# Patch copies of a deformable convolution issued from one queue, ahead of the stores, with the offsets' part of the schedule shifted

## What is computed

```python
# mixing, on g = group_norm(x), per image, p and q over the 1024 pixels
xn = g / max(norm_over_channels(g), 1e-8)
s  = relu(einsum('bcp,bcq->bpq', xn, xn)) ** 2
gx = einsum('oc,bcp->bop', W, g) + b
x1 = x + einsum('bpq,bcq->bcp', s, gx)
# deformable convolution, on h = group_norm(x1); 4 groups, 9 taps
offset = conv3x3(conv3x3(h, w1, b1), w2, b2)      # 4 * 9 * 2 = 72 channels
val    = bilinear samples of h at (pixel + tap + offset), zero outside
out    = x1 + relu(einsum('ogck,bgckhw->bohw', wd, val))
```

## Time and profile before

| what | value |
|---|---|
| median of three runs | 514.45 us |
| the profiled execution, its own time | 515.51 us |
| its span, first to last instruction | 513.8 us |
| TensorE (PE) busy | 428.8 us, 83% |
| VectorE (DVE) busy | 344.2 us, 67% |
| ScalarE (ACT) busy | 224.7 us, 44% |
| GpSimd (POOL) busy | 140.7 us, 27% |
| mean granted TensorE clock | 0.947 of full |

### The profile page before, as it was taken

How to read it: one execution, slowest core, us unless ns; L and a number is a source line. 1 busy time by engine, 2 the same in 40 slices (tenths; PEclk the granted TensorE clock), 3 DMA queues, 4 the chain that set the end, 5 groups by cost and what they waited for, 6 DMA issues and landing times.

```text
span 513.8 us, 9711 instructions
## 1 busy us (share of the span) xinstructions
PE 428.8 (83%) x3881; PEld 304.9 (59%) x3881; DVE 344.2 (67%) x582; ACT 224.7 (44%) x404; POOL 140.7 (27%) x179
## 2 busy tenths in 40 slices
PE   2899799967998988779998987878798976888886
PEld 2666465734665656557665654657565654666665
DVE  4619996499988983954657992745979538199400
ACT  2046133224565453414655453314765333178640
POOL 3266441343872102102763101101210101031100
PEclk9999799997999989989999989879998987999999
DMA  3400000201111113011101112011210121023211
GB/s 122 169 1 1 1 1 1 46 1 21 22 22 22 22 22 65 6 40 31 33 15 27 22 22 56 23 33 41 43 24 20 25 64 33 20 52 64 42 33 33
DMA packets 22187, 17.23 MB, mean 34 GB/s; under 512 B 1981, under 2 KB 20669, under 8 KB 22141
## 3 DMA queue, kind: packets, MB, share of 16 engines
q1 hardware_dynamic: 21884, 16.07, 12.9%
q10 hardware_dynamic: 256, 0.52, 0.7%
HBM read 3.74 MB, written 3.28 MB: 14 GB/s over the span
## 4 chain that ended last, share of the span: by engine, by line
PE 58%; DVE 24%; ACT 7%; issue 5%; DMA 3%; ACTq 2%; SPq 1%; DVEq 0%
PE psB L719 13%; PE psB L506 12%; PE psA L586 8%; DVE wpix L1342 6%; PE psV L695 5%; PE psA L506 5%; PE psT L672 5%; ACT wcell L897 3%; DVE tent L1323 2%; PE psT L662 2%; DMA hwin<-hwin 2%; PE psA L562 2%; DVE tent L1317 2%; DVE combo L1135 2%; ACT val L910 2%
## 5 line engine op out<-in xcount | busy, mean ns | idle before, releaser
L897 ACT ACTIVATE wcell<-psT 128x512 f32<-128x512 f32 (+1 forms) x160 | 83.4, 552 | 82.3 <-PE psT L672 73.6
L1342 DVE TENSOR_TENSOR wpix<-tent 128x512 f32<-128x512 f32 (+1 forms) x160 | 107.1, 720 | 16.0 <-PE psT L672 15.0
L672 PE MATMUL psT<-ident,wpix 128*128 128x128 f32 x576 | 86.5, 283 | 14.5 <-ACT wcell L897 13.5
L672 PEld LDWEIGHTS psT<-ident,wpix 128*128 128x128 f32 x576 | 66.9, 144 | 38.8 <-issue 28.7
L447 POOL COPY strips<-hring 128x256 f32<-128x256 f32 x64 | 43.3, 702 | 155.8 <-PE psT L662 155.8
L424 POOL TENSOR_TENSOR sim<-rel 128x512 f32<-128x512 f32 x48 | 60.3, 1276 | 62.4 <-ACT rel L858 62.4
L719 PE MATMUL psB<-val,wd_sb 128*128 128x256 f32 x288 | 73.5, 412 | 3.6 <-issue 3.6
L719 PEld LDWEIGHTS psB<-val,wd_sb 128*128 128x128 f32 x288 | 57.7, 206 | 15.6 <-issue 7.2
L695 PE MATMUL psV<-wcell,hwin 64*32 64x144 f32 x2048 | 48.5, 300 | 13.3 <-DMA hwin<-hwin 13.3
L910 ACT ACTIVATE val<-psV 128x576 f32<-128x576 f32 x64 | 44.0, 688 | 34.2 <-PE psV L695 22.7
L506 PE MATMUL psB<-g_p 128*128 128x512 f32 x144 | 44.6, 448 | 6.7 <-DVE g_p L1075 6.7
(11 more groups left out here) (166 smaller groups left out, 498.0 us busy)
## 6 DMA issues: line engine op xcount, KB each, us to landing
hwin<-hwin SPq DMA_DIRECT2D x64, 128.0 KB, 2.5
out<-yout SPq DMA_DIRECT2D x16, 128.0 KB, 1.8
x_all<-x SPq DMA_DIRECT2D x1, 1536.0 KB, 8.9
off_scr<-sim SPq DMA_DIRECT2D x4, 288.0 KB
combo<-sim SPq DMA_DIRECT2D x20, 32.0 KB
val<-w SPq DMA_DIRECT2D x1, 576.0 KB
wd_sb<-wd SPq DMA_DIRECT2D x1, 576.0 KB
x_all<-x SPq DMA_DIRECT2D x1, 512.0 KB, 3.5
```

The costliest lines, as they stand in the source:

```text
L672: last = pe.transpose(bank[:, at:at + P], wpix[:, t % 2, k, 2 * h:2 * h + 2, :].rearrange("p g q -> p (g q)"), ident[:, :])
L897: act.activation(wcell[:, t % 2, taps[0]:taps[-1] + 1, :, :].rearrange("q k h p -> q (k h p)"), bank[:, 0:len(taps) * G // 2 * P], ACT.Cop ...
L1342: dve.tensor_tensor(w, ty, tx, ALU.mult).then_inc(s["weights_done"], 1)
```

## The change

It does the following.

- SyncE issues the crossings of tiles 0 to 6 first, then all nine patch copies of the next batch and the save, the crossing of tile 7, and then all four stores. ScalarE issues patch copies only in the prologue.
- In `STEADY` the second convolution's combinations come one slot later, both convolutions' products (`conv`) come one slot later, and so do the output rows and the wrap; the turns of the offsets move from slots 60 and 61 to 64 and 66, and extremes from 66 to 69. The first weights of the next batch go from slot 62 to 66.
- In the prologue the extremes of batch 0 leave the table and are reduced at slot 12 of batch 0. Batch 2's diagonal goes to a buffer of its own (`ends_out`, which holds `orelu` and `yout` later), so it no longer waits for extremes. `high`, `low` and `diagonal` of batch 2 come one slot sooner, and some steps of batch 1's mixing come sooner.
- Batch 1's borrowed tiles are laid out in two halves by how long they are needed; the first evacuation of weights then waits for the mixing products, and only the one of tile 1 for the scaled sums.

```diff
-        LEAD = dict(mean=31, dev=31, var=33, norm=34, combine=(35, 46), high=(35, 46), conv=(40, 51), wrap=57,
-                    shift=57, turn={59: (0, 1), 61: (2, 3)}, extremes=65)
-        STEADY = dict(mean=23, dev=24, var=25, norm=28, combine=(29, 42), high=(30, 43), conv=(35, 48), wrap=54,
-                      shift=56, turn={60: (0, 1), 61: (2, 3)}, extremes=66)
+        LEAD = dict(mean=31, dev=31, var=33, norm=34, combine=(35, 46), high=(35, 46), conv=(40, 51), wrap=57,
+                    shift=57, turn={59: (0, 1), 61: (2, 3)}, extremes=None)
+        STEADY = dict(mean=23, dev=24, var=25, norm=28, combine=(29, 43), high=(30, 44), conv=(36, 49), wrap=55,
+                      shift=None, turn={64: (0, 1), 66: (2, 3)}, extremes=69)
...
-        SECOND = {26: (0,), 32: (3,), 34: (1, 2, 4), 38: (6,), 46: (7,), 49: (9,), 57: (10, 12, 13), 58: (15, 16),
+        SECOND = {26: (0,), 30: (3,), 34: (1, 2, 6), 35: (4,), 38: (7,), 49: (9,), 57: (10, 12, 13), 58: (15, 16),
                   60: (18, 19), 62: (21, 22), 63: (25,), 64: (26,)}
...
-        LEAD_WEIGHTS, FIRST_WEIGHTS = 60, 62
+        LEAD_WEIGHTS, FIRST_WEIGHTS, LEAD_EXTREMES = 60, 66, 12
...
                 sp.wait_ge(s["off_wrapped"], 2 * b + 2)
-                shift_taps(sp, range(BY_SYNC))
+                shift_taps(sp, range(K if b else BY_SYNC))
...
             for b in range(B):
-                for t in range(ROWT - 2):
+                for t in range(ROWT - 1):
                     cross(b, t)
                 if b + 1 < B:
                     shift_offsets(b + 1)
-                cross(b, ROWT - 2)
-                store(b, 0)
                 cross(b, ROWT - 1)
-                for m in range(1, 4):
+                for m in range(4):
                     store(b, m)
...
                 if b == 0 and t == 0 and idx == 0:
+                    act.wait_ge(s["mix_done"], 2 * QT)
+                if b == 0 and t == 1 and idx == 0:
                     act.wait_ge(s["scaled_done"], 4)
...
                 if what == "diagonal":
                     dve.wait_ge(s["inv2_done"], b + 1)
-                    if b >= 2:
+                    if b >= 3:
                         dve.wait_ge(s["extremes_done"], 2 * (b - 1))
```

More of the change, by code:

```diff
@@ L191, in mix_deform_kernel @@
         acc = spare[:, 2 * G * P + C:2 * G * P + C + K * P]
-        orelu = sb("orelu", [P, 2, HALF // 2])
-        yout = sb("yout", [P, 2, HALF // 2])
+        ends_out = sb("ends_out", [P, 2, HALF])
+        orelu, yout = (ends_out[:, i, :].rearrange("p (j n) -> p j n", j=2) for i in range(2))
         psT = pb("psT", [P, 2, BANK])
@@ L251, in mix_deform_kernel @@
                        27: ("diagonal",), 33: ("bias",)}
[L252 to L253 removed]
+        PREP_THIRD = {57: ("normalise", "square"), 58: ("norms", "invert"), 59: ("bias",), 63: ("high",), 64: ("low",),
+                      65: ("diagonal",)}
         PREP = {55: ("normalise", "square"), 57: ("high", "low"), 58: ("norms", "invert"), 59: ("bias",),
[L255 to L256 removed]
+                70: ("diagonal",)}
+        SECOND = {26: (0,), 30: (3,), 34: (1, 2, 6), 35: (4,), 38: (7,), 49: (9,), 57: (10, 12, 13), 58: (15, 16),
                   60: (18, 19), 62: (21, 22), 63: (25,), 64: (26,)}
@@ L1438, in batch_steps @@
                             add_out(b, 0)
+                        if b == 0 and n == LEAD_EXTREMES:
+                            find_extremes(0)
                         if b + 2 < B:
```

26 lines of the change are left out of this document (13 added, 13 removed).

## The result

The changed kernel takes 496.55 us (median of 4 runs, 494.72 to 498.97), the kernel before 514.20 beside it; the ratio is 0.9652 with a 95% interval of 0.9598 to 0.9707. That is 17.7 us less, where the forecast had 21.8 less, and the time lies inside the range. The profiled execution took 497.49 us, its span is 495.8, so against the profiled execution of before (515.51, span 513.8) the span is 18.0 shorter.

The account below looks back on a forecast made before the run. PE's own work, plus its standstills and lower clock, was taken as the bound. Terms 9.2 + 5.2 + 5.9 + 2.8 + 1.2 - 3.8 - 1.0 - 2.1 + 2.4 + 2.0 = 21.8 gave 492.6 us, range 487 to 504.

Parts of the forecast that it names:

- Stores behind the crossings: Last tile of a batch: shorter `hwin` waits gain 9.2 us, and no half clock behind them gains 5.2.
- The copies leave ScalarE: Around `dconv` 0: PE's wait gains 5.9 us, the slow first group 2.8, batch 0's waits 1.2.
- The new wait: PE waits for SyncE's nine patch copies before the offsets' turn: 1.9 us in batches 1 and 2, 3.8 lost.
- The windows' turns: Tiles 6 and 7: PE's wait of 0.40 ahead of the windows' turn goes, 2.4 us gained.
- Convolutions one slot later: Both convolutions: the wait of 0.94 grows to about 3.0, 2.23 becomes about 1.5; lag 0.7 per batch, 2.1 us lost.
- I set them equal: Convolutions: a clock fall behind the 3.0 us wait stands against the one before, so no net clock term.
- Batch 0's square: Batch 0: the square waits for output rows coming one turn and the lag later, 1.0 us lost.
- The end of the prologue: Prologue: extremes' move gains 2.3 us, exchanged mixing steps taken as -0.3; together 2.0 gained.
- the first: Rival: lengthened and shortened convolution waits both cool PE, 5 us more lost, 497.6 us; chance 0.2.
- The second: Rival: PE stays at 1.2 GHz from the new wait to the batch's end, 498 to 500.9 us; chance 0.1.
- The third: Rival: patch copies land 2 to 4 us later, PE waits in three batches, 499 to 505 us; chance 0.1.
- the fourth: Rival: SyncE's nine issues each take ScalarE's slowest 1.45 us, so slower, 518.2 us; chance 0.02.
- The fifth: Rival: tile 7's crossing waits for its windows behind the offsets' turn, 9.2 and 5.2 not gained, 507.0 us; chance 0.03.

Follow-up runs that it names:

- The single edit: Kernel before with only store 0 put behind tile 7's crossing: 501.39 us, ratio 0.9729.
- The list alone: Changed kernel with only the old table of batch 1's mixing steps in the prologue put back: 493.34 us, ratio 0.9552.
- the kernel with the old slots alone: Changed kernel with the convolutions' slots put back (combining 29 and 42, high half 30 and 43, convolution 35 and 48, wrap 54): 493.56 us, ratio 0.9563.
- the last kernel: Changed kernel with the old prologue mixing order and old convolution slots, plus the offsets' turns moved to slots 66 and 67: 490.04 us, ratio 0.9526.

## Why the prediction was right, and where not

Its sign, its bound (PE) and its main terms held; 17.7 us came where 21.8 were forecast. The terms that missed are the prologue's, batch 0's square and the convolutions', and the last two missed in opposite ways. Point by point, all from the profiled execution:

- *Stores behind the crossings*, 9.2 + 5.2: the four waits are 0.94, 0.94, 0.97 and 0.94, so 9.5 gained; sample and convolution behind them are back to 0.72 and 4.15 in three batches, 5.7 gained. The single edit gave 14.2 of the 14.4. Right.
- *The copies leave ScalarE*, 5.9 + 2.8 + 1.2: all three came. `dconv` 0, from its start to the next turn and without the turns among its groups, took 5.40 and 5.29 and now 3.99, so 1.4 and 1.3 gained, as forecast. Right, and shown to need the later turns beside it.
- *The new wait*, 1.9 in each of two batches, none in batch 0: measured 2.25, 1.85 and none. In batch 1 the issues were a little slower (0.73) and the landing a little sooner (1.8). It cost 1.4 us of clock in batch 1 (7.34 us from the turn to the tail's convolution, 322.53 to 329.87) and none in batch 2 (5.92, 410.02 to 415.94).
- *The windows' turns*, 2.4: the waits ahead of them in tiles 6 and 7 are gone. Right. Three of the six stand inside the convolutions' stretches measured here.
- *Convolutions one slot later*, a lag of 0.7 a batch: wrong in sign for two batches. It was 1.4 lost in the first convolution less 0.7 gained in the second. The first half was right: 1.47 and 1.46 lost in batches 0 and 1, and 3.03 in batch 2. The step that failed is the gain of 0.7 in the second, 1.1 with its wait ahead of the windows: it was 2.91, 2.62 and 2.83. Of that 1.5 in each batch is clock. "I set them equal" was said of the falls behind the two waits, but the one behind 2.23, seen before in all three batches (4.37, 4.00 and 4.46 for twelve matmuls that now take 3.4), did not come behind 1.51 in any.
- *Batch 0's square*, -1.0: mis-sized. From the windows' turn to the first part of `dconv` it is 12.13 instead of 8.17, so -4.0: the wait grew from 0.52 to 2.01, and 2.6 more went to the norms at half clock, which the term had left out. It is the price of the later slots.
- *The end of the prologue*, +2.0: this is the step that failed most. "The exchanged mixing steps fill PE's wait of 2.63", from +0.7 to -2.2, "taken -0.3". They did fill that wait (it is 0.97 now), but the mixing that they took away left PE with 0.70 us of work in the four from 78 to 82, a wait of 4.11 and half clock behind it (6.83 for 4.61), and GpSimd's squares came to lie beside VectorE's combinations and doubled them. The list alone gives 3.2 us back. The "2.3 gained" by the extremes was too much as well: they did leave VectorE's chain, but with the old list about 1.1 of it arrived. Batch 0 began 2.9 us later (126.77 for 123.91) instead of 2.0 earlier.

The same sum by stretches, which add up without a gap (us, from PE's start times in the two profiled executions; a loss is negative; the six waits ahead of the windows are split over the third and the sixth row):

| stretch | forecast | measured |
|---|---|---|
| start to the windows' turn in the middle of batch 0 (159.13, 162.70) | 2.0 | -3.6 |
| first convolutions, three batches | -4.2 | -6.0 |
| second convolutions, with the wait ahead of the windows behind them | 3.3 | 8.4 |
| from there to `dconv` 0: batch 0, with the square and norms | -1.0 | -4.0 |
| the same in batches 1 and 2 (the copies leave ScalarE) | 5.9 | 6.0 |
| `dconv` 0 to the tail's `dconv`: `hwin` waits, slow groups, new wait | 12.1 | 13.2 |
| the tail's `dconv` and the sample behind it | 3.7 | 4.3 |
| everything else | 0 | -0.3 |
| sum | 21.8 | 18.0 |

So it is partly luck that the total missed by only 3.8: 5.6 too much in the first row and 4.8 in the second and fourth stand against 5.1 too little in the third.

Of the rivals, the first (the convolutions lose 5 us more by the clock) came with 1.1 us in two batches, and the second convolution's clock gave back more than that. The second did not come: behind the wait of 2.25 the sample at 323.70 was slow, but the convolution at 329.87 ran at 4.15; turns and samples alone brought the clock back. So what the prediction quoted from the Trainium skill (TensorE: Matmul & The Clock Gate, Part 4) on transposes does not decide this kernel's time; the trace speaks against it, as far as turns and samples together can. (The upper end of that rival adds up to 500.8, not 500.9.) The third was off because a patch is usable 1.8 us behind its issue, and the fourth because nine in a row cost 0.73 and 0.68 each. The fifth fell with the tail's waits.

## What to carry to other kernels

Look first for a queue in which something late stands ahead of something needed: one store behind a crossing instead of ahead of it gave 14 of 18 us. When issues are moved to another queue, the consumer has to move with them, or a wait only changes its name; and each entry put ahead of another delays that one, so the queue's own order is to be costed both ways. Work that seems free to move earlier can be the only thing between an engine and its next wait, and can land beside an engine that it slows, as GpSimd's squares did with VectorE's sums: ask what an interval will hold once the work is gone, not only where it goes.

## What was not expected of the hardware

- VectorE's sum of two operands in SBUF (128x544) takes 0.71 to 0.80 us with GpSimd idle and 1.45 to 1.56 beside GpSimd's squares and copies.
- One slot's move of a wait kept the clock behind it: 1.51 us instead of 2.23 ahead of the second convolution, and that convolution's part takes 16.25 to 16.31 us in all 21 batches seen, at granted clock 1.00 in the changed kernel, where it took 18.89 to 19.18 before, at 0.91.
- A wait does not have one price. PE kept its clock behind 2.75 us in the prologue and lost it behind 4.11, and behind 2.01 in batch 0 (norms 6.55 for 3.98). The same wait in the same place goes either way: at the turn of the offsets the changed kernel lost 1.4 us behind 2.25 (batch 1) and nothing behind 1.85 (batch 2), the kernel with the old slots alone nothing behind 2.33 (5.93 us from the turn to the tail's convolution) and 1.5 behind 1.85 (7.42). So a clock term of this size is not to be forecast from the wait's length alone; the runs of one experiment's kernel here spread by 1.5 to 6.8 us.
- Taking the wait for the copies away entirely, as the last kernel did, gave nothing measurable: 2.6 us in batches 1 and 2 against 1.7 lost in batch 0 to a chain of PE and VectorE.
